# Four image layers on one core: another TensorE order in the third layer's loop, another order of mixing, convolution and loads in the last stage

## The chip, the cores and the metric

The kernel runs on one core of one Trainium2 chip. The metric is the time of one execution in microseconds (us); the median of three executions of the kernel before is 4027.63 us (4027.61 to 4030.76). The rows below come from one profiled execution. PE is the TensorE matmul, DVE VectorE, ACT ScalarE, POOL GpSimd, SP the engine that issues nearly all DMAs.

## The reference, cut to what matters

Four residual layers over x of 8 images x 32 channels x 128 x 128, float32. The change touches the third and the fourth.

```python
x = x + _L0_conv_ref(_gn(x), ...)
x = x + _L1_conv_ref(_gn(x), ...)
x = x + _L2_conv_ref(_gn(x), ...)   # layer 3 here: attention
x = x + _L3_conv_ref(_gn(x), ...)   # layer 4 here: global * local

# _L2: channel mean, a 5x5 difference of Gaussians, a 3x3 Sobel pair, then
#   return x * (1.0 + ALPHA * sigmoid(mag * gate_w[0] + gate_b[0]))
# _L3:
c_ft = jnp.fft.rfft2(c)
top = jnp.einsum('bixy,ioxy->boxy', c_ft[:, :, :m, :m], w1)
bot = jnp.einsum('bixy,ioxy->boxy', c_ft[:, :, -m:, :m], w2)
...
g = jnp.fft.irfft2(out_ft, s=(h, w))
l = y + conv_b          # y: a 3x3 convolution with wrapped borders
return g * l
```

## The kernel before

All five engines run one program each and wait on semaphores that count up. The order of the work on an engine is the order in which its program is written; no scheduler moves anything.

The first 3140 us (layers 1 and 2) are not touched, but for two semaphores that are merged. Then come the **tails**, a loop over t from -2 to 8 on PE and ACT (`for t in range(-2, B + 1)`), with its counterparts on DVE (over i), POOL and SP. An iteration handles three images at once: the attention of image t+1, the norm and forward DFT of image t, and the last layer's 3x3 convolution of image t-1. Its steps, for one image:

- POOL `tail_sum` (L1172) adds layer 2's result; DVE `group_stats` (L1196) takes the statistics; `group_means` (L551) and `group_vars` (L558) are PE products that sum them, between them DVE `group_deviations`; ACT `group_root` (L902) and DVE `group_scale` finish a norm, and ACT `normalise` (L908) writes the normed image into `xn3`. gn2 is the norm ahead of the attention, gn3 the one ahead of the last layer.
- PE `gray_sum` (L788) sums the channels, ACT copies the sum (L1064), PE `blur` (L749), ACT copies it (L1069), PE `sobel` (L755, L757), ACT squares and takes the root (L1078), and later the tanh (L1086); DVE `attend` (L1486, L1489) applies the attention and takes gn3's statistics.
- PE `dft_rows` (L766) and `dft_columns` (L778) transform the image; ACT `dft_out` (L1038) and `spectrum` (L1045) copy the results.
- DVE `bands` (L1512 to L1514) transposes the normed image into one of the two buffers `cpad`; POOL adds the border rows (L1185, L1186, `halo_ready`); PE `conv3` (L568) convolves it in two halves of 9 taps; a half takes all four PSUM banks 0 to 3, so ACT `conv3_out` (L1052) has to evacuate one half before the next starts. SP `bands_out` (L488) stores the result to `l3_dram`; the attended image is stored to `x3_dram` (L495).

conv3 is cut into parts of taps (`TAP_PARTS`) that are laid between the four quarters of gray_sum and of dft_rows.

Behind the loop comes the **last stage**. PE mixes the spectra of all images with the weights `wm` (L846), into banks 0 to 3, after the last convolution. ACT copies the result to `ys` (L1099), SP stores it to `spec_dram` in 32 DMAs (L522) and loads it back in another layout (L525). Then for each image ACT copies its slice (L1105), PE does the inverse DFT in two steps (L859, ACT L1110, L870), DVE multiplies with the convolution's result in `le` and adds the attended image in `xe` (L1551, L1553), and SP stores `xe` as output (L540). `xe` and `le` have two buffers each, and SP's loop takes the images in pairs: loads of both (L535, L311), then the two stores.

## Time and profile before

| | |
|---|---|
| profiled execution, its own time | 4031.34 us |
| its span | 4029.5 us |
| median of three executions | 4027.63 us |
| mean granted TensorE clock | 0.909 |
| busy: PE, DVE, POOL, ACT | 3360.5, 2853.2, 2344.2, 1851.4 us |
| DMA queue of kind instruction | 287 packets, 4.70 MB |
| layers 1 and 2 | until about 3140 us |
| tails and last convolution | 3140 to 3712 us |
| mixing of the spectra | 3712 to 3772 us |
| spectrum stored and loaded, inverse DFT, output | 3772 to 4029.5 us |

A line of the timeline reads: start, length in us, engine, line of the program, operation, out<-in, shapes, number of instructions, and in brackets the idle time of the engine ahead of it with what ended it. "issue" there means that the engine waited for nothing that the profile shows. The profile counts a float32 matmul twice. Granted clock 1.00 is 2.4 GHz, 0.50 is 1.2 GHz.

### The profile page before, as it was taken

What the parts mean: (1) busy time and instruction counts of PE and PEld (TensorE: products, weight loads), DVE (VectorE), ACT (ScalarE), POOL (GpSimd) and SP (SyncE); (2) the same over time, 40 slices, a digit from 0 to 9 for tenths busy, and PEclk for the clock granted to TensorE, in tenths of its full rate; (3) what the DMA queues carried; (4) which work ended last, traced back from release to release, by engine and by line L of the source; (5) the groups of instructions that cost most, each with busy time, mean ns of one, the idle gap of its engine ahead of it and who ended that gap; (6) DMA issues with size and microseconds to landing.
All of it is one profiled execution on the core that took longest, in us unless ns stands there. A gap on an engine that the chain in (4) does not pass through costs nothing.

```text
span 4029.5 us, 90064 instructions
## 1 busy us (share of the span) xinstructions
PE 3360.5 (83%) x32900; PEld 1182.2 (29%) x32900; DVE 2853.2 (71%) x3513; ACT 1851.4 (46%) x2702; POOL 2344.2 (58%) x1131
## 2 busy tenths in 40 slices
PE   5669999569999999999999999999999568776444
PEld 2334444212212222222222222222222345454433
DVE  3652554379989989899899999899999654542034
ACT  0115556445555545555455555555555455552010
POOL 0000000069999999999999999999999432301000
PEclk9889999779999999999999999999999778787555
DMA  7574898666656666666656666666666544415487
GB/s 161 126 157 97 168 184 171 154 143 153 143 137 155 150 143 144 147 148 152 144 138 155 151 144 148 139 157 149 149 148 159 135 126 117 137 54 117 104 213 205
DMA packets 495588, 586.47 MB, mean 146 GB/s; under 512 B 72354, under 2 KB 335138, under 8 KB 489819
## 3 DMA queue, kind: packets, MB, share of 16 engines
q1 hardware_dynamic: 484596, 563.66, 61.0%
q10 hardware_dynamic: 10560, 16.93, 1.7%
q8 instruction: 287, 4.70, 0.5%
q14 instruction: 145, 1.19, 0.1%
HBM read 409.91 MB, written 184.54 MB: 148 GB/s over the span
## 4 chain that ended last, share of the span: by engine, by line
POOL 30%; PE 29%; issue 27%; DMA 4%; DVE 4%; ACT 3%; SPq 2%; ACTq 0%; POOLq 0%; DVEq 0%
POOL arena L1153 26%; PE ps L568 7%; PE ps L609 7%; PE ps L616 4%; PE ps L680 3%; DMA arena<-l_dram 2%; PE ps L766 2%; POOL arena L1141 2%; ACT arena L908 1%; PE ps L870 1%; PE ps L662 1%; PE ps L788 1%; DVE arena L1551 1%; PE ps L846 1%; DMA arena<-x_dram 1%
## 5 line engine op out<-in xcount | busy, mean ns | idle before, releaser
L1153 POOL TENSOR_TENSOR arena<-arena 128x1024 f32<-128x1024 f32 x896 | 1932.1, 2198 | 553.6 <-ACT arena L1011 553.6
L1464 DVE TENSOR_TENSOR arena<-ps,arena 128x1024 f32<-128x1024 f32 x1792 | 2107.0, 1219 | 203.9 <-PE ps L662 172.7
L680 PE MATMUL ps<-arena,w_mix 128*32 128x512 f32 x10752 | 1437.9, 607 | 79.6 <-POOL arena L1153 79.6
L1011 ACT ACTIVATE arena<-ps 128x1024 f32<-128x1024 f32 x896 | 918.8, 1025 | 1025.1 <-PE ps L672 1014.2
L662 PE MATMUL ps<-arena,sel 48*128 48x512 bf16 x3584 | 701.9, 385 | 24.3 <-issue 15.6
L662 PEld LDWEIGHTS ps<-arena,sel 48*128 48x128 bf16 x3584 | 190.1, 93 | 944.4 <-issue 936.0
L568 PE MATMUL ps<-arena,w_conv 32*32 32x512 f32 x9216 | 368.6, 674 | 74.8 <-POOL arena L1186 34.5
L672 PE MATMUL ps<-norms,opw 57*128 57x512 bf16 x1792 | 348.1, 384 | 49.1 <-ACT arena L943 17.5
L680 PEld LDWEIGHTS ps<-arena,w_mix 128*32 128x32 f32 x10752 | 214.3, 108 | 467.5 <-issue 467.5
L908 ACT ACTIVATE arena<-arena,nmr,rstd 128x128 f32<-128x128 f32 x768 | 300.5, 481 | 33.0 <-DVE arena L1514 30.4
L609 PE MATMUL ps<-arena,circ 128*128 128x512 f32 x640 | 288.0, 595 | 14.4 <-ACT arena L922 14.4
L1185 POOL COPY arena<-arena 32x130 f32<-32x130 f32 x32 | 39.1, 1221 | 373.2 <-DVE arena L1514 372.2
L568 PEld LDWEIGHTS ps<-arena,w_conv 32*32 32x32 f32 x9216 | 169.3, 109 | 216.5 <-issue 130.2
L672 PEld LDWEIGHTS ps<-norms,opw 57*128 57x128 bf16 x1792 | 101.7, 93 | 435.3 <-issue 429.9
L1551 DVE TENSOR_TENSOR arena<-arena,ps 128x512 f32<-128x512 f32 x64 | 43.7, 682 | 253.2 <-DMA arena<-l_dram 210.0
L1136 POOL TENSOR_TENSOR arena<-arena 128x1024 f32<-128x1024 f32 x62 | 133.1, 2146 | 95.9 <-ACT arena L952 95.9
L616 PE MATMUL ps<-arena,circ 128*128 128x512 f32 x384 | 176.3, 594 | 0.0
L609 PEld LDWEIGHTS ps<-arena,circ 128*128 128x128 f32 x640 | 120.3, 189 | 167.0 <-issue 167.0
L1196 DVE BATCH_NORM_STATS2 st<-arena 128x6 f32<-128x128 f32 x768 | 156.6, 279 | 7.1 <-POOL arena L1172 4.9
L870 PE MATMUL ps<-k,arena 64*128 64x128 f32 x512 | 59.9, 422 | 111.5 <-DVE arena L1551 111.5
L1129 POOL TENSOR_TENSOR col<-col,powers 128x1 f32<-128x1 f32 x8 | 4.4, 552 | 243.4 <-DVE col L1252 243.4
L1392 DVE TENSOR_TENSOR arena<-arena 128x512 f32<-128x512 f32 x64 | 44.3, 693 | 143.0 <-ACT arena L927 141.0
(151 smaller groups left out, 2223.9 us busy)
## 6 DMA issues: line engine op xcount, KB each, us to landing
arena<-pad SPq DMA_DIRECT2D x768, 260.0 KB, 7.7
split_dram<-arena SPq DMA_DIRECT2D x64, 768.0 KB, 3.6
arena<-split_dram SPq DMA_DIRECT2D x1536, 32.0 KB, 3.1
x_dram<-arena SPq DMA_DIRECT2D x16, 2048.0 KB, 7.9
l_dram<-arena SPq DMA_DIRECT2D x128, 256.0 KB, 3.9
arena<-l_dram SPq DMA_DIRECT2D x32, 1024.0 KB, 14.8
arena<-x_dram SPq DMA_DIRECT2D x16, 2048.0 KB, 14.0
pad<-arena SPq DMA_DIRECT2D x8, 2080.0 KB, 16.6
```

The source lines that it names most:

```text
L568: m = pe.matmul(ps[C * j:C * j + C, bank + g, :], weights[C * g:C * g + C, dy, dx, :], tile[C * g:C * g + C, r:r + CR, dx:dx + W], start=t ...
L609: m = pe.matmul(ps[:, n % 2, :], circ[:, d, :], yp[h % 2][:, 4 * n:4 * n + 4, 4 - d:4 - d + W], start=d == 0, stop=d == 4)
L616: m = pe.matmul(ps[:, 2 + n % 2, :], circ[:, 5 + d, :], yp[h % 2][:, 4 * n:4 * n + 4, 4 - d:4 - d + W], start=d == 0, stop=d == 2)
L662: m = pe.matmul(ps[:, 2 * (n % 2) + e, :], sel[ROWS2 * e:ROWS2 * e + SPLIT_ROWS, u % GROUP, :], split[ROWS2 * e:ROWS2 * e + SPLIT_ROWS, pa ...
L672: m = pe.matmul(ps[:, POOL_BANK + e, :], opw[ROWS2 * e:ROWS2 * e + KROWS, SPREAD[c], :], norms[ROWS2 * e:ROWS2 * e + KROWS, buf, half, :]. ...
L680: m = pe.matmul(ps[C * g:C * g + C, SUM + chunk % 2, :], w_mix[:, s, :], ring[:, (first + g // 2) % size, NPX * (g % 2):NPX * (g % 2) + NP ...
L908: m = nc.scalar.activation(tile[:, c, :], src[:, c, :], ACT.Identity, scale=rstd[:, gn.slot + n % 2, c:c + 1], bias=nmr[:, gn.slot + n % 2 ...
L1011: nc.scalar.activation(ring_p[:, slot, :], ps[:, POOL_BANK:POOL_BANK + 2, :].rearrange("p a n -> p (a n)"), ACT.Tanh).then_inc(tanh_p, 1)
L1136: nc.gpsimd.tensor_tensor(rest, tt, hml[:, 0, :], ALU.subtract).then_inc(rows_r, 1)
L1153: nc.gpsimd.tensor_tensor(slot, slot, pixels(chunk % 2, SPREAD[n // 2], n % 2), ALU.mult).then_inc(prod_p, 1)
L1196: m = nc.vector.bn_stats(st[:, c, :], tile[:, c, :])
L1464: nc.vector.tensor_tensor(slot, weights, pixels(par, ONCE[n // 2], n % 2), ALU.mult).then_inc(prod_d, 1)
```

## The change

1. In the tails' loop on PE the first half of an iteration holds conv3 of image t-2, second half (`conv3(t - 2, 1)`), where it held image t-1, first half; the second half of the iteration holds image t-1, first half. The taps are cut 3+3+3 and end ahead of the fourth quarter, where they were cut 2+2+2+3 with the last behind it.
2. `group_means` of gn3 stands ahead of blur, `group_vars` between blur and sobel; they stood behind blur and behind sobel.
3. ACT's `conv3_out` and SP's `bands_out` follow that order; SP issues `x1_in` for a later image ahead of the stores of the convolution's first half, and the weights `wm` at the start of the last iteration but one.
4. Mixing stands ahead of the two halves of image 7's convolution and writes banks 4 to 7. conv3_out of image 7 stands on ACT behind the copies of the mixed spectrum, and PE waits for it ahead of the inverse DFT.
5. The spectrum is stored by 8 DMAs. `xe` and `le` have three buffers each, at new addresses; the loads of images 0 and 1 and `x3` of image 2 are issued ahead of the spectrum's store. Behind each output store come `l3_in(b + 3)` and then `x3_in(b + 2)`.
6. SP's and DVE's last loops are unrolled. bias0_loaded and w3_loaded are merged into const_loaded and shift_loaded.

```diff
-        ys = part(37640, 2048).rearrange("p (a b m) -> p a b m", a=8, b=B)
+        ys = part(37512, 2048).rearrange("p (a b m) -> p a b m", a=8, b=B)
...
-        xe = [planes(0), planes(24704)]
-        le = [planes(4096), planes(16384)]
+        xe = [planes(0), planes(20480), planes(24576)]
+        le = [planes(4096), planes(16384), planes(32068)]
...
             for t in range(B):
+                if t == B - 1:
+                    weights_in()
                 sp.wait_ge(x3_done, 4 * (t + 1))
                 sp.dma_start(x3_dram[t], xd[t % 3]).then_inc(x3_stored[t % 3], 16)
-                if t >= 1:
-                    bands_out(t - 1, 0)
+                if t >= 2:
+                    bands_out(t - 2, 1)
...
+            for half in range(2):
+                sp.wait_ge(l3_stored[half], 64 * (B - 2))
+            sp.wait_ge(x3_stored[(B - 3) % 3], 16 * ((B - 3) // 3 + 1))
+            l3_in(0)
+            l3_in(1)
+            sp.wait_ge(gn3.out, 4 * B)
+            sp.wait_ge(x3_stored[(B - 1) % 3], 16 * ((B - 1) // 3 + 1))
+            x3_in(0)
+            sp.wait_ge(bands_ready, B)
+            sp.wait_ge(dfth_mm, 4 * B)
+            x3_in(1)
+            bands_out(B - 2, 1)
+            sp.wait_ge(conv3_mm, 2 * (B - 1))
+            x3_in(2)
...
+            for half in range(HALVES):
+                bands_out(B - 1, half)
+            for half in range(2):
+                sp.wait_ge(l3_stored[half], 64 * B)
+            l3_in(2)
+
+            for b in range(B):
+                sp.wait_ge(out_done, START + 8 * (b + 1))
+                sp.dma_start(image(out, b), xe[b % 3]).then_inc(out_stored[b % 3], 16)
+                if b + 3 < B:
+                    l3_in(b + 3)
+                if 1 <= b and b + 2 < B:
+                    sp.wait_ge(out_stored[(b - 1) % 3], START + 16 * ((b - 1) // 3 + 1))
+                    x3_in(b + 2)
...
-            TAP_PARTS = ((0, 1), (2, 3), (4, 5), (6, 7, 8))
+            TAP_PARTS = ((0, 1, 2), (3, 4, 5), (6, 7, 8))
             for t in range(-2, B + 1):
                 for n in range(4):
                     if 0 <= t + 1 < B:
                         gray_sum(t + 1, n)
-                    if t >= 1:
-                        conv3(t - 1, 0, TAP_PARTS[n])
...
+                    if t >= 2 and n < 3:
+                        conv3(t - 2, 1, TAP_PARTS[n])
...
                 for n in range(4):
-                    if t >= 1:
-                        conv3(t - 1, 1, TAP_PARTS[n])
+                    if 1 <= t < B and n < 3:
+                        conv3(t - 1, 0, TAP_PARTS[n])
...
             pe.wait_ge(dftw_copy, 3 * B)
+            mix_spectrum()
+            for half in range(HALVES):
+                conv3(B - 1, half, range(TAPS))
             pe.wait_ge(conv3_evac, 2 * B)
...
+            for half in range(HALVES):
+                conv3_out(B - 1, half)
             act.wait_ge(spec_loaded, 16)
```

PE's program in iteration t = 6, from the gray sums (L788 before, L811 in the changed kernel; the order counts a float32 matmul once), before:

```order
1699 L788 MATMUL ps<-arena,ident 128x128 x8
1700 L568 MATMUL ps<-arena,w_conv 32x512 x32
1701 L788 MATMUL ps<-arena,ident 128x128 x8
1702 L568 MATMUL ps<-arena,w_conv 32x512 x32
1703 L788 MATMUL ps<-arena,ident 128x128 x8
1704 L568 MATMUL ps<-arena,w_conv 32x512 x32
1705 L788 MATMUL ps<-arena,ident 128x128 x8
1706 L568 MATMUL ps<-arena,w_conv 32x512 x48
1707 L749 MATMUL ps<-gray,k 128x128 x5
1708 L551 MATMUL ps<-st,k 128x32 x2
1709 L755 MATMUL ps<-dog,k 128x128 x2
```

and after:

```order
1683 L811 MATMUL ps<-arena,ident 128x128 x8
1684 L591 MATMUL ps<-arena,w_conv 32x512 x48
1685 L811 MATMUL ps<-arena,ident 128x128 x8
1686 L591 MATMUL ps<-arena,w_conv 32x512 x48
1687 L811 MATMUL ps<-arena,ident 128x128 x8
1688 L591 MATMUL ps<-arena,w_conv 32x512 x48
1689 L811 MATMUL ps<-arena,ident 128x128 x8
1690 L574 MATMUL ps<-st,k 128x32 x2
1691 L772 MATMUL ps<-gray,k 128x128 x5
1692 L581 MATMUL ps<-dev,k 128x32 x2
1693 L778 MATMUL ps<-dog,k 128x128 x2
```

The convolution (L568, now L591) ends ahead of the last gray sum, and gn3's mean (L551, now L574) stands ahead of blur (L749, now L772).

PE's program from the columns of image 7's DFT (L778 before) to the last loop, before:

```order
1732 L778 MATMUL ps<-k,arena 32x32 x64
1733 L568 MATMUL ps<-arena,w_conv 32x512 x288
1734 L846 MATMUL ps<-cs,arena 32x16 x1024
1735 L850 UNCONDITIONAL_BRANCH
1736 L850 ISA
```

and after:

```order
1711 L801 MATMUL ps<-k,arena 32x32 x64
1712 L591 MATMUL ps<-arena,w_conv 32x512 x144
1713 L867 MATMUL ps<-cs,arena 32x16 x1024
1714 L591 MATMUL ps<-arena,w_conv 32x512 x288
1715 L878 UNCONDITIONAL_BRANCH
```

One half of a convolution (image 6's second) now stands ahead of mixing (L846, now L867), and the two of image 7 behind it.

SP's issues from the last store of `x3_dram`, before:

```order
595 L495 DMA x_dram<-arena 128x4096
596 L488 DMA l_dram<-arena 128x1x512 x8
597 L513 DMA arena<-in_w1r 32x32x64 x4
598 L513 DMA arena<-in_w1i 32x32x64 x4
599 L513 DMA arena<-in_w2r 32x32x64 x4
600 L513 DMA arena<-in_w2i 32x32x64 x4
601 L488 DMA l_dram<-arena 128x1x512 x8
602 L522 DMA spec_dram<-arena 32x256 x32
603 L525 DMA arena<-spec_dram 32x8192
604 L531 UNCONDITIONAL_BRANCH
```

and after:

```order
598 L513 DMA x_dram<-arena 128x4096
599 L488 DMA l_dram<-arena 128x1x512 x8
600 L311 DMA arena<-l_dram 64x32x128 x4
601 L504 DMA arena<-x_dram 128x4096 x2
602 L488 DMA l_dram<-arena 128x1x512 x4
603 L504 DMA arena<-x_dram 128x4096
604 L545 DMA spec_dram<-arena 32x4x256 x8
605 L548 DMA arena<-spec_dram 32x8192
606 L488 DMA l_dram<-arena 128x1x512 x8
607 L311 DMA arena<-l_dram 64x32x128 x2
608 L557 DMA out<-arena 128x32x128
```

The weights stand ahead of this piece now; five image loads stand ahead of the spectrum's store, and image 7's bands and `l3` of image 2 behind the spectrum's load.

## Rows read from the trace of the kernel before

**Rows 1.** Timeline, PE, iteration t = 3 (start, us, what; idle before in brackets)

```profile
3383.30 3.56 PE L568 MATMUL ps<-arena,w_conv 32*32 32x512 f32 x64 [2.84 <-POOL arena L1186]
...
3395.31 2.05 PE L788 MATMUL ps<-arena,ident 128*128 128x128 f32 x16
...
3409.59 3.24 PE L766 MATMUL ps<-k,arena 128*128 128x64 f32 x16 [2.50 <-ACT arena L908]
3412.76 4.08 PE L568 MATMUL ps<-arena,w_conv 32*32 32x512 f32 x64
...
3423.39 3.40 PE L568 MATMUL ps<-arena,w_conv 32*32 32x512 f32 x96
...
3428.56 0.58 PE L558 MATMUL ps<-dev,k 128*128 128x32 f32 x4
```

**Rows 2.** Timeline, ACT, the same iteration

```profile
3400.73 2.12 ACT L1052 ACTIVATE arena<-ps,bias 128x1024 f32<-128x1024 f32 x2 [3.07 <-PE ps L568]
...
3425.49 1.28 ACT L902 ACT_TABLE_LOAD   x1
3429.41 0.23 ACT L902 ACTIVATE root<-sd 128x32 f32<-128x32 f32 x1 [2.64 <-DVE sd L1216]
```

**Rows 3.** Timeline, DVE, where iterations t = 3 and 4 begin

```profile
3365.25 8.02 DVE L1512 STREAM_TRANSPOSE arena<-arena 128x4096 f32<-128x4096 f32 x1
...
3430.17 8.03 DVE L1512 STREAM_TRANSPOSE arena<-arena 128x4096 f32<-128x4096 f32 x1
```

**Rows 4.** Timeline, all engines, iteration t = 1: gn3's statistics and its normalise

```profile
3252.90 6.27 DVE L1196 BATCH_NORM_STATS2 st<-arena 128x6 f32<-128x128 f32 x32
...
3276.46 2.02 ACT L908 ACTIVATE arena<-arena,nmr,rstd 128x128 f32<-128x128 f32 x5
```

**Rows 5.** Timeline, all engines, from image 7's statistics to mixing

```profile
3637.31 6.33 DVE L1196 BATCH_NORM_STATS2 st<-arena 128x6 f32<-128x128 f32 x32
...
3656.65 6.26 ACT L908 ACTIVATE arena<-arena,nmr,rstd 128x128 f32<-128x128 f32 x16 [0.65 <-DVE nmr L1223]
...
3678.98 2.12 PE L778 MATMUL ps<-k,arena 128*32 128x32 f32 x128 [0.68 <-ACT arena L1038]
...
3698.25 10.86 PE L568 MATMUL ps<-arena,w_conv 32*32 32x512 f32 x288 [2.21 <-ACT arena L1052]
...
3712.24 1.96 PE L846 MATMUL ps<-cs,arena 32*32 32x16 f32 x122 [3.13 <-DMA arena<-in_w2i]
```

**Rows 6.** Timeline, PE: two bursts of layer 1's convolution, two of mixing

```profile
203.90 4.43 PE L568 MATMUL ps<-arena,w_conv 32*32 32x512 f32 x127 [1.45 <-issue]
212.54 4.47 PE L568 MATMUL ps<-arena,w_conv 32*32 32x512 f32 x66 [4.21 <-issue]
...
3721.28 2.06 PE L846 MATMUL ps<-cs,arena 32*32 32x16 f32 x128 [2.51 <-issue]
...
3751.24 2.06 PE L846 MATMUL ps<-cs,arena 32*32 32x16 f32 x128 [1.69 <-issue]
```

**Rows 7.** Timeline, all engines, from the spectrum's store to image 1's first product

```profile
3773.99 14.91 SPq L522 DMA_DIRECT2D spec_dram<-arena  x32
...
3798.08 1.04 ACT L1105 COPY arena<-arena 32x1024 f32 x1 [24.11 <-DMA arena<-spec_dram]
...
3806.34 4.41 PE L870 MATMUL ps<-k,arena 64*128 64x128 f32 x32
...
3815.06 0.69 DVE L1551 TENSOR_TENSOR arena<-arena,ps 128x512 f32<-128x512 f32 x1 [134.21 <-DMA arena<-l_dram]
...
3832.01 0.69 DVE L1551 TENSOR_TENSOR arena<-arena,ps 128x512 f32<-128x512 f32 x1 [3.16 <-PE ps L870]
```

**Rows 8.** Last stage: image 2's first product; a stretch (last: clock, DMA share, GB/s); landing

```profile
3871.11 0.69 DVE L1551 TENSOR_TENSOR arena<-arena,ps 128x512 f32<-128x512 f32 x1 [25.27 <-DMA arena<-l_dram]
...
3904.60:3943.00 38.40, 11.46 (x156) 10.43 (x158) 10.18 (x16) 1.22 (x3) 0.00 (x0) 0.50 1.08 272
...
out<-arena SPq DMA_DIRECT2D x5, 2048.0 KB, 8.7
```

More of the change, by code:

```diff
@@ L289, in four_layers @@
         wm_loaded, spec_mm, spec_copy, spec_stored, spec_loaded = (once(n) for n in ("wm_loaded", "spec_mm", "spec_copy", "spec_stored", "spec_loaded"))
-        xe_loaded, le_loaded, out_stored = two("xe_loaded", sem), two("le_loaded", sem), two("out_stored", sem)
+        xe_loaded, le_loaded, out_stored = ([sem(f"{n}{i}") for i in range(3)] for n in ("xe_loaded", "le_loaded", "out_stored"))
         slice_done, idfth_mm, idfth_copy, idftw_mm, out_mul, out_done = (sem(n) for n in (
@@ L520, in _ @@
                 for q in range(4):
-                    for xx in range(4):
-                        sp.dma_start(spec_dram[MODES * t + 4 * q + xx],
-                                     ys[C * q:C * q + C, 4 * t + xx, :, :].rearrange("p b m -> p (b m)")).then_inc(spec_stored, 16)
-            sp.wait_ge(spec_stored, 16 * KX)
+                    first = MODES * t + 4 * q
+                    sp.dma_start(spec_dram[first:first + 4].rearrange("x o m -> o x m"),
+                                 ys[C * q:C * q + C, 4 * t:4 * t + 4, :, :].rearrange("p x b m -> p x (b m)")).then_inc(spec_stored, 16)
@@ L541, in _ @@
-            for par in range(2):
-                sp.wait_ge(out_stored[par], START + 16 * B // 2)
+            for half in range(HALVES):
[11 more added lines that the diff above has]
+                    x3_in(b + 2)
@@ L544, in _ @@
+            for b in range(B - 3, B):
+                sp.wait_ge(out_stored[b % 3], START + 16 * (b // 3 + 1))
         @block.tensor
@@ L570, in conv @@
                 return m
[L572 removed]
+            pe.wait_ge(const_loaded, 32)
             pe.wait_ge(init_done, 1)
@@ L817, in _ @@
                 if 0 <= t + 1 < B:
-                    sobel(t + 1)
+                    blur(t + 1)
                 if 0 <= t < B:
                     group_vars(gn3, t)
+                if 0 <= t + 1 < B:
+                    sobel(t + 1)
                 for n in range(4):
-                    if t >= 1:
-                        conv3(t - 1, 1, TAP_PARTS[n])
+                    if 1 <= t < B and n < 3:
+                        conv3(t - 1, 0, TAP_PARTS[n])
                     if 0 <= t < B:
@@ L1064, in _ @@
                     nc.scalar.copy(gray[:, 2:W + 2], ps[:, 5, 0:W]).then_inc(gray_done, 1)
-                if t >= 1:
-                    conv3_out(t - 1, 0)
+                if t >= 2:
+                    conv3_out(t - 2, 1)
                 if 0 <= t + 1 < B:
@@ L1090, in _ @@
                     dft_out(t, 3)
-                if t >= 1:
-                    conv3_out(t - 1, 1)
+                if 1 <= t < B:
+                    conv3_out(t - 1, 0)
                 if 0 <= t < B:
```

111 lines of the change are left out of this document (49 added, 62 removed).

## The prediction

> **What bounds the kernel now.** I read the page's busy shares by slice first: the first 3140 us are two layers whose code stays as it is, so only the last 890 us can move. There I read the chain of waits and then each engine's timeline.
>
> In the tails the iterations repeat every 64.92 us, counted between two starts of DVE's transposes in bands [rows 3]. No engine is full. PE starts cold, waits 2.84 us for image t-1's border rows from POOL [rows 1], and ends its first half with a part of the convolution behind the last gray sum. ACT evacuates that convolution (2.12 us) ahead of its copies for blur and sobel [rows 2], and the norm of the attended image, gn3, waits behind all this. So the loop is one ring: bands, gray sums with convolution, evacuation, sobel, gn3, DFT rows with convolution, gn2, bands.
>
> Between tails and output lies one serial string: two halves of image 7's convolution, mixing, the spectrum through DRAM, slices. PE mixes for 59.4 us, from 3712.24 [rows 5] to 2.3 us ahead of the spectrum's store at 3773.99 [rows 7] (ACT's copies). That is no arithmetic: a burst of 128 rows takes 2.06 us, then PE stands 1.69 us at "issue" [rows 6], so one burst costs 3.75 us. The page lists a queue of kind instruction, 287 packets and 4.70 MB (in the table above), 16 KB each, and I take the gaps for waits on such a packet.
>
> In the last stage DVE waits 25 us for data once in each pair of images [rows 8], and PE and ACT wait for DVE. When data is there, an image takes 16.95 us [rows 7].
>
> **The change part by part.** Times are counted from the start of bands in an iteration.
>
> *Steady iterations, t = 2 to 6.* The last gray sum ended at 3397.36 [rows 1]; conv3_out began at 3400.73 [rows 2]. Now that sum has 96 more counted matmuls ahead of it (3.40 us warm [rows 1]), less the 2.84 us for border rows that are long there, so it ends 0.56 us later, and I take 0.4, since PE warms up sooner without that pause. But conv3_out starts 0.35 us behind it and no more 3.37 us: net 2.6 us earlier, and so are sobel and gn3. With the mean and variance ahead of sobel, the root no longer waits for them: 0.2 us. Together 2.8 us. The second half has the first DFT quarter where it was against normalise (3409.59), then 192 counted matmuls of convolution and not 224 up to gn2's variance. But they sit differently: 32 more ahead of the third quarter's end in each of two parts (1.1 us each: at 1.2 GHz 64 take 4.08 us, later 96 take 3.40 [rows 1]), and none behind it. Before, the variance (3428.56 [rows 1]) released the root at 3429.41 [rows 2]; now ACT does, which loads two tables behind the third quarter and is ready at 3426.77 [rows 2], 17.2 us after the first quarter's start. 17.2 + 2.2 = 19.4 us against 19.8 before: 0.4 us more. An iteration gains some 3.2 us, five 16.0 us. Bounds: 0, if another wait takes over; 6.3, if PE, which now rests 1.6 us and not 2.50 ahead of the first quarter [rows 1], keeps 2.4 GHz there (quarter 2.0 us and not 3.24, 96 matmuls 3.4 and not 5.2).
>
> *Iteration 1* has no convolution in its first half any more. gn3's statistics end at 3259.17 and normalise starts at 3276.46, 17.3 us later [rows 4]. What remains of that is mean, blur, two ACT copies, sobel and root, 5.7 us worked out from the same instructions elsewhere in the trace. Gain 11.6, with the second half's share 12.0 us.
>
> *Iteration 7* convolves in its first half what is long there, while DVE still takes statistics. Statistics end at 3643.64, normalise starts at 3656.65, 13.0 us later [rows 5]; mean, deviations, variance, table and root need 5.9: gain 7.1. Its second half loses 32 counted matmuls: 1.1. Together 8.2 us.
>
> *Mixing starts earlier.* Between the end of the DFT's columns (3681.10) and mixing's start lie 31.1 us of border rows and two halves of convolution [rows 5]. One half of 10.86 us remains: 20.3 us. The weights are issued some 9 us into iteration 7 and lie there by 40 us; mixing begins at about 63, so they hide (before, mixing waited 3.13 us for the last of them [rows 5]).
>
> Mixing so begins 12.0 + 16.0 + 8.2 + 20.3 = **56.5 us** earlier.
>
> *Mixing under load.* New beside it: five image loads of 2.1 MB and a store of 1 MB, 11.5 MB, at 272 GB/s [rows 8] 42 us, of which about 36 fall into mixing. Its instructions come by the same DMA engines. In layer 1, where the DMAs were nearly full, two bursts of 128 lie 8.64 us apart [rows 6]; under the last weights and stores a burst of mixing lay 2.06 + 2.51 = 4.57 us behind the one before [rows 6]. In 36 us, bursts of 4.57 us lose 36 x (1 - 3.75/4.57) = 6 us, bursts of 8.64 lose 20. I take 12, nearer the middle, since the image loads are as dense as layer 1's: **-12 us**.
>
> The Trainium skill (Runtime: NRT & Kernel Launch, Instruction fetch mechanics) says that crossing a 16 KiB block is mostly hidden. The trace does not agree for these short matmuls, 1.69 us stand open at each; by the rule the term would be 0 and the time 12 us less.
>
> *From the spectrum's store on.* Let R be that store's start, 3773.99 before; the kernel ended at R + 255.5. Now PE convolves image 7 from R - 2.3: 12.1 us (10.86 and 1.3 for a cold start, 64 in 3.56 against 96 in 3.40 [rows 1]), evacuation 2.2, 10.9, evacuation 2.2: R + 25.1. The spectrum is back sooner: eight issues, 0.47 to 0.8 us each (14.91/32 [rows 7]; the stores of a quarter MB cost the latter), and not 14.91 us. So the convolution decides. Before, the slice was copied at R + 24.1 and the first product was possible 12.7 us later, at 3810.75 [rows 7]; it waited for `le` until R + 41.1. Now it is due at R + 25.1 + 12.7 = R + 37.8, images 0 and 1 loaded. An image done 13.8 us later (16.95 less the 3.16 for PE [rows 7]): image 0 at R + 51.6, 1 at 68.6, 2 at 85.6.
>
> From then on DMA decides. One store and four loads, 10.5 MB, took 38.4 us at 272 GB/s, DMA share 1.08 [rows 8], so an image's 6.3 MB cost 23.1 us, above 16.95. The batch behind image b is its store, l3 of b+3, x3 of b+2; the first has no x3. It starts at 51.6 and takes 15.4. Then four of 23: 68.6 to 91.6, 114.6, 137.6, 160.6, and one without l3 to 176. x3 of image 3 is there at 91.6, x3 of 6 at 160.6, image 6 done at 160.6 + 1.5 + 13.8 = 176, image 7 at 193, its store landed (8.7 [rows 8]) at **R + 202**. Gain 255.5 - 202 = **53.5 us**. Bounds: 181 were DMA free (17 us an image), 230 did an image cost the 29 us that it takes now.
>
> *Hidden.* Three x3 stores and bands that move in SP's queue have 15 us and more of slack: POOL reads its loads 18 us into an iteration. Merged semaphores wait for transfers that are long done. Unrolled loops need a few instruction packets on DVE and SP, 0 to 5 us, inside the range.
>
> **The sum**: 56.5 - 12 + 53.5 = 98.0 us. The profiled execution took 4031.34 us (span 4029.5), 3.7 above the median. Against the median: 4027.6 - 98.0 = 3929.6, I say 3930.
>
> **The rivals.**
>
> *The last stage stays at its pace.* Loads and stores now alternate image by image, and SP waits for a store ahead of x3. If an image then costs 29 us, the output ends at R + 230, the time is 3958. For it: x3(b+2), which is needed next, queues behind l3(b+3), which is not. Against: DMA never runs dry, since a batch is issued 7 us and more ahead of the end of the one before.
>
> *Mixing starves.* 20 us and a few for the half of convolution beside the loads: 3940 to 3950. For it: an x3 row of 16 KB is one piece. The Trainium skill (DMA: Bandwidth & Descriptors, Queues, rings and completion order) has each DMA engine take turns between queues a packet at a time, so an instruction packet waits for a whole one of the loads; layer 1's 8.64 us would agree. Against: the stores and weights beside mixing cost only 0.82 us a burst [rows 6].
>
> *The tails keep 64.9 us*, since a chain that I took for slack (ACT's copies, DVE's second statistics) is next: no 16.0, 3946.
>
> *PE stays at 2.4 GHz in the second half*: 15 us more gain, 3915.
>
> *Slower than before*: five batches would have to cost 100 us more than I count, 43 us an image, that is 6.3 MB at 146 GB/s. It would need stores and loads of neighbouring images to hinder each other that much; the stretch of [rows 8] holds a store and loads at 272. Above 4028 only if it falls under that 146.
>
> *The change does not do what it says*: the program order shows it in place, so this has no chance of its own.
>
> **How the numbers follow.** The forecast, 3930 with 12 us to both sides, 0.50; last stage at its pace 0.14; mixing starves 0.14; faster clock 0.12; tails unchanged 0.07; slower 0.03. The range 3902 to 3960 takes in all but the slow case and combinations of two. Some 0.2% (8 us) is what a measurement of this kernel tells from no change; all cases but one lie far below: faster 0.96, same 0.01, slower 0.03.
>
> **What would show it.** Tails: starts of bands 61.7 us apart; no wait for POOL at the first convolution. Normalise of gn3 6 us behind its statistics in iterations 1 and 7. Mixing: total 71 us and not 59.4, its gaps longer while x3 loads run. First product 38 us behind the spectrum's store, with no wait for `le`. From image 3 on, first products 23 us apart, DMA share near 1. The prediction is wrong where images come every 17 or 29 us, or mixing takes over 85.

## The result, and the profile after

The changed kernel takes 3923.6 us (median of 4 runs, 3922.26 to 3929.7) against 4027.93 us before, measured again beside it: a ratio of 0.9742, 95% interval 0.9726 to 0.9759. The forecast was 3930, with 3902 to 3960 as range. The profiled execution took 3922.26 us with a span of 3920.1, 109.4 less than the span before.

The page of the changed kernel, in parts: busy times, the slices of PE's clock and of the DMAs, the instruction queue.

```profile
PE 3338.9 (85%) x32900; PEld 1184.0 (30%) x32900; DVE 2855.7 (73%) x3513; ACT 1849.5 (47%) x2702; POOL 2341.5 (60%) x1131
...
PEclk9899999879999999999999999999999967888665
DMA  6574898566656656666666666666666664535589
...
q8 instruction: 287, 4.70, 0.5%
```

The matmuls (32900), the instruction packets (287) and the bytes are what they were. PE is busy 3338.9 us and not 3360.5, which is 21.6 of the 109.4 us; the rest are waits that went. The last two of the 40 slices move 191 and 251 GB/s, where 213 and 205 stood before.

Timeline of PE in iteration 3, which answers to [rows 1] (start, us, what, idle before and its releaser):

```profile
3356.82 3.57 PE L811 MATMUL ps<-arena,ident 128*128 128x128 f32 x15 [9.19 <-ACT arena L936]
...
3360.53 4.41 PE L591 MATMUL ps<-arena,w_conv 32*32 32x512 f32 x96
...
3381.40 3.41 PE L591 MATMUL ps<-arena,w_conv 32*32 32x512 f32 x96
3386.36 2.00 PE L789 MATMUL ps<-k,arena 128*128 128x64 f32 x16 [1.56 <-ACT arena L936]
3388.29 3.41 PE L591 MATMUL ps<-arena,w_conv 32*32 32x512 f32 x96
```

In the tails no matmul waits for POOL any more. The pause ahead of the first DFT quarter is 1.56 us and not 2.50; that quarter takes 2.00 us and not 3.24, and 96 matmuls behind it 3.41 us, where 64 took 4.08. The granted clock (third number from the end of a line below) of the convolution behind the quarter says the same, in the kernel before, in the changed one, and in iteration 4 of the changed one:

```profile
3412.80:3416.80 4.00, 4.00 (x66) 1.01 (x65) 0.00 (x0) 3.67 (x9) 0.00 (x0) 0.50 1.21 202
...
3388.36:3391.70 3.34, 3.34 (x98) 1.40 (x97) 0.71 (x4) 3.34 (x9) 0.00 (x0) 1.00 1.19 206
...
3448.00:3453.00 5.00, 5.00 (x98) 1.90 (x97) 0.78 (x5) 4.65 (x12) 0.00 (x0) 0.66 1.21 197
```

So behind the first quarter PE keeps 2.4 GHz in iteration 3, where it had fallen to 1.2 GHz before. It does not in every iteration: in the last line the 96 matmuls take 5.01 us at a mean of 0.66, though the pause ahead of the quarter was 1.55 us there too. The transposes in bands, which answer to [rows 3], where iterations 2, 3 and 4 begin:

```profile
3345.37 8.04 DVE L1542 STREAM_TRANSPOSE arena<-arena 128x4096 f32<-128x4096 f32 x1
3406.43 8.03 DVE L1542 STREAM_TRANSPOSE arena<-arena 128x4096 f32<-128x4096 f32 x1
3466.01 8.02 DVE L1542 STREAM_TRANSPOSE arena<-arena 128x4096 f32<-128x4096 f32 x1
```

Iterations 2 to 6 take 58.0, 61.1, 59.6, 57.5 and 55.9 us, where 65.0, 64.9, 64.9, 64.9 and 60.3 stood. The spread is new. In iteration 3 PE stops for 2 us within the third part of the convolution:

```profile
3397.84 2.17 PE L591 MATMUL ps<-arena,w_conv 32*32 32x512 f32 x43 [2.04 <-issue]
```

Every profile that has both the new order of the convolution and its cut into 3+3+3 has such a stop in iteration 3, of 0.45 to 2.67 us, and nearly all have one in iteration 4. What causes it was not tried.

Mixing in PE's timeline (five of the first bursts, and one later), for [rows 6], and the issues of the spectrum's store and load in SP's queue:

```profile
3648.28 2.05 PE L867 MATMUL ps<-cs,arena 32*32 32x16 f32 x128 [6.36 <-issue]
3657.78 2.05 PE L867 MATMUL ps<-cs,arena 32*32 32x16 f32 x128 [7.45 <-issue]
3663.99 2.05 PE L867 MATMUL ps<-cs,arena 32*32 32x16 f32 x128 [4.16 <-issue]
3669.93 2.06 PE L867 MATMUL ps<-cs,arena 32*32 32x16 f32 x128 [3.89 <-issue]
3676.14 2.05 PE L867 MATMUL ps<-cs,arena 32*32 32x16 f32 x128 [4.16 <-issue]
...
3690.85 2.05 PE L867 MATMUL ps<-cs,arena 32*32 32x16 f32 x128 [1.70 <-issue]
```

```profile
3719.86 4.75 SPq L545 DMA_DIRECT2D spec_dram<-arena  x8
3726.41 0.32 SPq L548 DMA_DIRECT2D arena<-spec_dram  x1
```

Stretches (us, busy time and count of PE, PEld, DVE, ACT, POOL; clock, DMA share, GB/s):

```profile
3640.00:3680.00 40.00, 12.29 (x743) 11.36 (x728) 0.00 (x0) 2.12 (x2) 0.00 (x0) 0.58 0.98 270
3680.00:3720.00 40.00, 23.88 (x1379) 21.46 (x1395) 0.00 (x0) 2.31 (x8) 0.00 (x0) 0.50 0.02 5
...
3745.00:3770.00 25.00, 19.64 (x297) 18.32 (x301) 10.49 (x16) 4.40 (x8) 0.00 (x0) 0.57 0.71 127
...
3820.00:3840.00 20.00, 11.40 (x192) 10.53 (x192) 8.44 (x14) 3.07 (x5) 0.00 (x0) 0.59 1.16 274
```

While loads fill the DMAs (share 0.98), PE stands 4 to 7.5 us between bursts of 128; in the second half of mixing the DMAs are idle (0.02) and the gaps are what they were. First products of images 0, 1, 2, 3 and 4 on DVE, for [rows 7, 8]:

```profile
3756.02 0.69 DVE L1580 TENSOR_TENSOR arena<-arena,ps 128x512 f32<-128x512 f32 x1 [124.07 <-PE ps L898]
...
3775.36 0.69 DVE L1580 TENSOR_TENSOR arena<-arena,ps 128x512 f32<-128x512 f32 x1 [5.41 <-PE ps L898]
...
3794.71 0.69 DVE L1580 TENSOR_TENSOR arena<-arena,ps 128x512 f32<-128x512 f32 x1 [5.40 <-PE ps L898]
...
3815.58 0.69 DVE L1580 TENSOR_TENSOR arena<-arena,ps 128x512 f32<-128x512 f32 x1 [6.93 <-DMA arena<-x_dram]
...
3837.68 0.69 DVE L1580 TENSOR_TENSOR arena<-arena,ps 128x512 f32<-128x512 f32 x1 [8.34 <-DMA arena<-x_dram]
```

The last two of the stretches lie in the last stage; from 3820 to 3840 the DMAs are full (share 1.16). The wait of 25 us in each pair of images is gone; 7 to 8 us in each of images 3 to 6 remain, for x3.

### The profile page after: what moved, and what is told of

Same layout as the page of the kernel before. It is cut to its first block, busy times and chain, and to the rows that moved or that the text cites. A ratio compares the mean times of both kernels' runs of the same rounds, so it can differ in the third digit from the quotient of the medians.

```text
span 3920.1 us, 89862 instructions
## 1 busy us (share of the span) xinstructions
PE 3338.9 (85%) x32900; PEld 1184.0 (30%) x32900; DVE 2855.7 (73%) x3513; ACT 1849.5 (47%) x2702; POOL 2341.5 (60%) x1131
## 4 chain that ended last, share of the span: by engine, by line
PE 30%; POOL 29%; issue 28%; DVE 5%; ACT 4%; DMA 2%; SPq 1%; ACTq 0%; POOLq 0%; DVEq 0%
POOL arena L1183 27%; PE ps L591 8%; PE ps L632 7%; PE ps L639 4%; PE ps L703 3%; POOL arena L1171 2%; ACT arena L936 2%; PE ps L789 1%; PE ps L811 1%; DVE arena L1542 1%; PE ps L685 1%; PE ps L898 1%; PE ps L867 1%; DMA arena<-x_dram 1%; DMA w_conv<-in_conv_w 1%
## 5 line engine op out<-in xcount | busy, mean ns | idle before, releaser
L591 PE MATMUL ps<-arena,w_conv 32*32 32x512 f32 x9216 | 354.0, 650 | 42.6 <-issue 34.3
L591 PEld LDWEIGHTS ps<-arena,w_conv 32*32 32x32 f32 x9216 | 179.1, 107 | 178.8 <-issue 125.5
L811 PE MATMUL ps<-arena,ident 128*128 128x128 f32 x512 | 78.8, 319 | 70.0 <-ACT arena L936 69.9
```

The costliest lines, as they stand in the source:

```text
L591: m = pe.matmul(ps[C * j:C * j + C, bank + g, :], weights[C * g:C * g + C, dy, dx, :], tile[C * g:C * g + C, r:r + CR, dx:dx + W], start=t ...
```

## The experiments

Each kernel's one profile was cut at the same marks: T, the first transposes in bands, bands(0), where iteration 1 begins; bands(1) and bands(6), where iterations 2 and 7 begin; the first matmul of mixing; R, the first store of the spectrum; the end. All in us, worked out as differences of such rows; the median is of all runs of the kernel:

| kernel | T | iteration 1 | iterations 2 to 6, mean | bands(6) to mixing | mixing to R | R to end | T to end | median |
|---|---|---|---|---|---|---|---|---|
| before | 3235.2 | 65.1 | 64.0 | 92.0 | 61.8 | 255.5 | 794.3 | 4027.9 |
| changed | 3233.9 | 53.5 | 58.4 | 60.5 | 79.9 | 200.2 | 686.2 | 3923.6 |
| changed_again | 3245.2 | 53.5 | 59.3 | 60.2 | 77.5 | 197.0 | 684.3 | 3928.6 |
| tails_only | 3240.7 | 53.1 | 58.2 | 90.7 | 62.2 | 256.8 | 753.9 | 3993.4 |
| last_only | 3232.8 | 65.2 | 64.0 | 61.7 | 76.9 | 201.9 | 725.8 | 3960.2 |
| norm_order_undone | 3230.8 | 51.0 | 58.9 | 60.4 | 81.0 | 200.0 | 686.8 | 3920.6 |
| four_parts | 3234.2 | 55.4 | 60.5 | 60.5 | 78.5 | 201.1 | 698.0 | 3941.7 |
| before_filler | 3240.7 | 63.7 | 62.9 | 87.5 | 61.1 | 255.8 | 782.3 | 4021.4 |
| quiet_mixing | 3236.2 | 53.2 | 58.3 | 59.6 | 60.5 | 216.9 | 681.4 | 3922.8 |
| l_in_mixing | 3244.6 | 53.5 | 58.8 | 60.5 | 70.4 | 196.5 | 674.6 | 3918.8 |
| x_in_mixing | 3240.3 | 53.2 | 58.9 | 59.6 | 67.1 | 203.9 | 678.4 | 3921.1 |
| three_in_mixing | 3241.9 | 53.5 | 58.6 | 60.3 | 76.7 | 197.5 | 680.7 | 3918.8 |
| two_buffers | 3232.4 | 53.5 | 58.5 | 60.4 | 76.4 | 203.1 | 685.7 | 3925.1 |
| combined | 3236.8 | 51.5 | 59.2 | 60.9 | 70.9 | 194.0 | 673.1 | 3909.7 |

T varies by 14 us between profiles, though ahead of it only the order of a few instructions differs. So differences of a few us are read from T on, and a median alone tells little below 10 us.

**The changed kernel again.** The kernel unchanged, beside the last three.

> The changed kernel itself, measured again beside the next three: 3920 to 3925. Its profile gives the distance from the first transposes in bands to the end once more; 686 us as in the first profile, if the spread between runs of some us comes from the two layers ahead of that point.

3928.61 us (3922.47 to 3935.03, 5 runs), above what was expected; T to end 684.3, 1.9 less than in the first profile, while T itself came 11.3 us later. The difference between the two profiles does come from ahead of T. Its parts are not that steady: iteration 3 took 65.3 us here and 61.1 there (a stop of 2.67 us, and PE at half rate behind it), while mixing was 2.4 and R to end 3.2 us shorter. So the mean iteration is good to some 1 us, mixing and R to end to some 3.

**The tails alone.** In short:

```
+            for half in range(HALVES):
+                conv3(B - 1, half, range(TAPS))
             pe.wait_ge(wm_loaded, 16 * 16)
             pe.wait_ge(dftw_copy, 3 * B)
+            pe.wait_ge(conv3_evac, 2 * B)
             mix_spectrum()
-            for half in range(HALVES):
-                conv3(B - 1, half, range(TAPS))
-            pe.wait_ge(conv3_evac, 2 * B)
```

and the buffers, loads and output loop of the kernel before.

> The changed PE, ACT and SP order of the tails alone; image 7's convolution ahead of mixing, two buffers and the output loop as in the kernel before. In the changed kernel's profile the DFT's columns of image 7 end 51.3 us earlier than before, and here three halves of convolution follow (6's second, 7's two, some 35 us with their evacuations) instead of two and the wait for border rows (31.1 us). So mixing starts some 47 us earlier, takes 59.4 us, and all behind it is as before: 3980. Rival: part of the 51.3 us comes from the last stage's edits, such as the transfers that no more stand in SP's queue; then this gains less, 3990 or more.

3993.39 us (ratio 0.9914, 0.9896 to 0.9932): 13 us above the expected, and where the rival had it. T was 5.5 us later than before; from T on it gains 40.4. Iterations 1 to 6 gain as in the changed kernel (12.0 and 29.0), but from bands(6) to mixing only 1.3 us are left, where I had expected 6: the third half of convolution and its waits take more than I gave them. The DFT's columns end 50.4 us behind bands(6), as in the changed kernel (50.3; before 60.8), so the rival's reason does not hold; from there to mixing it is 40.4 us, where I had counted 35 and the kernel before has 31.1.

**The last stage alone.**

```
-            TAP_PARTS = ((0, 1, 2), (3, 4, 5), (6, 7, 8))
+            TAP_PARTS = ((0, 1), (2, 3), (4, 5), (6, 7, 8))
...
-                    if t >= 2 and n < 3:
-                        conv3(t - 2, 1, TAP_PARTS[n])
+                    if 1 <= t < B:
+                        conv3(t - 1, 0, TAP_PARTS[n])
```

with the rest of the tails' order as before (the second half of convolution, the norm, ACT's and SP's order).

> The order of the tails as in the kernel before, the last stage changed: mixing directly behind the DFT's columns, both halves of image 7's convolution behind it, three buffers loaded during it. 31 us less ahead of mixing, 18 more in it (77.6 us for 59.4, as the changed kernel's profile shows), 55 less from the spectrum's store on: 4028 - 68 = 3960. The two parts then sum to 116 us where both together gave 104, since the wait for image 7's border rows (7 us) and evacuations are hidden by either. Rival: the gains of the last stage hang on the tails' order (border rows late, mixing starved more): 3975 or more.

3960.18 us (ratio 0.9825, 0.9802 to 0.9848), as expected; 68.5 us from T on. With the tails' 40.4 that makes 108.9, and both together gave 108.1 and 110.0. The parts simply add; the overlap of 12 us that I expected does not exist.

**The norm's order undone.**

```
+                if 0 <= t + 1 < B:
+                    blur(t + 1)
                 if 0 <= t < B:
                     after(pe, dftw_copy, 3 * t)
                     group_means(gn3, t)
                 if 0 <= t + 1 < B:
-                    blur(t + 1)
+                    sobel(t + 1)
                 if 0 <= t < B:
                     group_vars(gn3, t)
-                if 0 <= t + 1 < B:
-                    sobel(t + 1)
```

> The changed kernel with gn3's means behind the blur and its variance behind sobel again; the convolution's halves stay where the change has them. Theory: the pause of PE ahead of the first DFT quarter grows from 1.56 us to about 2.5 us, the granted clock falls again, the quarter takes 3.2 us and not 2.0, the 96 matmuls behind it 5.2 and not 3.4: 3.3 us in each of six iterations, 3943. Rival: the clock is kept by what PE does ahead (96 instead of 64 matmuls, no wait for border rows), and the order of the norm is worth 0.2 us each: 3925.

3920.64 us (ratio 0.9738, 0.9716 to 0.9760), T to end 686.8: no difference. The theory behind 3943 falls, and the trace says why; PE in iteration 3:

```profile
3375.94 3.40 PE L591 MATMUL ps<-arena,w_conv 32*32 32x512 f32 x96
3380.79 2.00 PE L789 MATMUL ps<-k,arena 128*128 128x64 f32 x16 [1.45 <-ACT arena L936]
```

The pause is 1.45 us with the old order and 1.56 with the new: 96 matmuls (3.40 us) stand ahead of the quarter where 64 (2.35 us) stood. What shortened the pause is the new cut of the convolution, not the order of the norm. In iteration 1 the new order even loses 2.4 us (53.5 against 51.0).

**Four parts.** The next run changes only that cut.

```
-                    if 1 <= t < B and n < 3:
-                        conv3(t - 1, 0, TAP_PARTS[n])
+                    if 1 <= t < B:
+                        conv3(t - 1, 0, ((0, 1), (2, 3), (4, 5), (6, 7, 8))[n])
```

> The changed kernel, with the convolution half beside the DFT in four parts (64, 64, 64, 96 matmuls) as before the change instead of three of 96; the other half keeps its three. Theory: PE's pause ahead of the first DFT quarter sets the clock. 64 instead of 96 matmuls there make it 2.5 us and not 1.56, the granted clock falls, the quarter takes 3.2 us and not 2.0 and the part behind it runs at half speed: 3 us an iteration, 3940. Rival: the clock is kept by what comes earlier (no wait for border rows, 96 matmuls in the first half): the pause is 2.5 us, the quarter 2.0 us all the same, and the time 3925.

```profile
3386.73 2.35 PE L591 MATMUL ps<-arena,w_conv 32*32 32x512 f32 x64
3391.68 3.67 PE L789 MATMUL ps<-k,arena 128*128 128x64 f32 x16 [2.60 <-ACT arena L936]
3395.28 3.71 PE L591 MATMUL ps<-arena,w_conv 32*32 32x512 f32 x64
```

3941.69 us (ratio 0.9794, 0.9767 to 0.9820), 12 to 14 us more from T on. In all five steady iterations the pause is 2.60 or 2.61 us and the quarter takes 3.67 or 3.68; in the changed kernel the pause is 1.55 or 1.56 and the quarter 2.00, though what PE does in the first half is the same in both. An iteration costs 1.2 to 2.1 us more on the mean, less than the 3 expected. It is not less everywhere: iterations 2 and 5 take 61.3 and 61.4 us, 3.3 to 4.3 more than in the two profiles of the changed kernel. But iterations 3 and 4 are hardly longer, since the changed kernel loses time there by its stops at "issue" and four_parts has none, and iteration 6 costs 1 us more.

**More work in the kernel before.**

```
+                if 1 <= t < B - 1:
+                    for _ in range(16):
+                        pe.matmul(ps[:, 6, 0:W], sobm[:, 0, :], dog[:, 0:W], start=True, stop=True)
```

> The kernel before, with 16 matmuls of 128 columns added behind gn3's variance in iterations 1 to 6; they write a PSUM bank that the first DFT quarter overwrites, so this is added work alone. Theory: the pause ahead of that quarter shrinks from 2.5 to about 1.5 us, PE keeps 2.4 GHz, the quarter takes 2.0 us and not 3.2, the part behind it half the time: 2 to 3 us an iteration less by more work, 4012 to 4016. Rival: the clock falls for what came earlier (the wait for border rows), and nothing changes: 4028.

```profile
3408.52 3.82 PE L823 MATMUL ps<-dog,k 128*128 128x128 f32 x32
3412.27 2.35 PE L568 MATMUL ps<-arena,w_conv 32*32 32x512 f32 x64
3414.55 2.00 PE L766 MATMUL ps<-k,arena 128*128 128x64 f32 x16
3416.47 2.35 PE L568 MATMUL ps<-arena,w_conv 32*32 32x512 f32 x64
```

4021.43 us (ratio 0.9986, 0.9974 to 0.9998), and 12.0 less from T on. The theory had 4012 to 4016, the rival 4028. The added matmuls count double, as 32, and take 3.82 us, so they fill the whole pause of 2.5 us and 1.3 us more; the quarter takes 2.00 us and not 3.2, and the part behind it 2.35 and not 4.1, both at a granted clock of 1.00 (from 3414.55 to 3418.80). An iteration is 1.15 us shorter with 3.8 us more work in it, where 2 to 3 us were expected. From bands(6) to mixing it is 4.5 us shorter too, though nothing was added in iteration 7; its pause is 1.44 us and not 1.96, and its first quarter 2.00. An exact fill was not tried. The wait for border rows (2.84 us) is still in this kernel, and the clock holds all the same, so that wait was not the cause. What these runs do not tell apart is the length of the pause and the amount of work just ahead of it: each run that changed one changed the other.

**No loads in mixing.** All of l3_in(0), l3_in(1), x3_in(0) to x3_in(2) moved behind the spectrum's load:

```
             sp.dma_start(arena[0:KX, 8192:8192 + C * B * 2 * MODES], spec_dram.rearrange("x o m -> x (o m)")).then_inc(spec_loaded, 16)
+            for half in range(2):
+                sp.wait_ge(l3_stored[half], 64 * (B - 1))
+            l3_in(0)
+            x3_in(0)
+            l3_in(1)
+            x3_in(1)
+            x3_in(2)
```

> The changed kernel, but the loads of images 0 and 1 and of x3 of image 2 are issued behind the spectrum's load and not during mixing. Theory: mixing's 18 extra us are instruction packets that wait behind the loads' packets. Then mixing takes 59 to 62 us, the spectrum's store comes some 17 us earlier; the 42 us of loads then run from 9 us behind that store to 51 us behind it, ahead of the first image's end, so only the convolution of image 7 pays some us for its own instructions: 3911. Rival 1: mixing is slow for another reason (what precedes it, the weights, the stores of bands): 3925 to 3940. Rival 2: the last stage is bound by bytes, so what mixing gives the stage takes back: 3922.

```profile
3646.53 2.05 PE L867 MATMUL ps<-cs,arena 32*32 32x16 f32 x128 [1.70 <-issue]
...
3810.77 0.69 DVE L1580 TENSOR_TENSOR arena<-arena,ps 128x512 f32<-128x512 f32 x1 [18.32 <-DMA arena<-x_dram]
```

3922.82 us (ratio 0.9742, 0.9724 to 0.9760). Mixing falls from 79.9 to 60.5 us: its extra time was the loads, shown. But from R on it takes 216.9 us, 16.7 more: image 3 waits 18.3 us for its x3, whose load stands behind those of convolved images 3 and 4. The second rival came true; of the 17 to 19 us saved in mixing only 3 to 5 stay from T on.

**Two loads of either kind in mixing.** In l_in_mixing only l3_in(0) and l3_in(1) stay there, in x_in_mixing only x3_in(0) and x3_in(1).

> The changed kernel, with only the convolved images 0 and 1 (4.2 MB) loaded during mixing and the x3 of images 0 to 2 issued behind the spectrum's load. Theory: 42 us of loads cost mixing 19.4 us (77.2 against 57.8 with none), so 15.5 us of loads cost some 7; and the last stage is bound by bytes (with all loads behind the spectrum it took 217 us from the spectrum's store on), of which this moves 15.5 us into mixing, whose second half leaves the DMAs idle. So mixing 65 us, end at the store's start + 201, 3909. Rival: the last stage gives back whatever mixing gains, here too: 3921. Rival on packets: the 512-byte rows of these loads disturb the instructions more, mixing 70 us or more.

> The same with the x3 of images 0 and 1 (4.2 MB, packets of 16 KB) loaded during mixing and the convolved images behind the spectrum's load. Theory that only the time of the loads counts: as with the convolved images, mixing 65 us and 3909. Theory that an instruction packet waits for whole packets of the loads: the large packets cost more, mixing 68 to 72 us and 3913 to 3917, and the run beside it less.

3918.76 us (ratio 0.9732, 0.9703 to 0.9761) and 3921.09 us (the same ratio and interval). From T on 674.6 and 678.4, 10 to 12 and 6 to 8 less than the changed kernel. Two DMA views of 10 us of mixing, 3655 to 3665 in l_in_mixing (GB/s by slice, packets) and 3650 to 3660 in x_in_mixing (packets):

```profile
GB/s 188 178 172 166 176 178 186 205 236 152 156 145 145 145 215 276 299 299 281 223 201 203 199 199 195 193 201 195 186 193 186 190 211 217 248 279 285 277 264 215
DMA packets 4081, 2.09 MB, mean 209 GB/s; under 512 B 32, under 2 KB 4080, under 8 KB 4080
```

```profile
DMA packets 744, 3.44 MB, mean 344 GB/s; under 512 B 94, under 2 KB 94, under 8 KB 597
```

The convolved image travels in packets of some 512 bytes at some 200 GB/s. In the second view 147 packets are over 8 KB, the rows of x3, among smaller ones of the stores, at 344 GB/s. Mixing's gaps reach 5.81 us under the former and 4.44 under the latter, and it takes 9.9 and 6.6 us more than with none: the large packets are not the worse ones. The changed kernel has both: gaps of 6.4 and 7.5 us while the DMAs move some 200 GB/s (the convolved images), then 3.9 to 4.2 us at 400 GB/s and more (x3). The Trainium skill (DMA: Bandwidth & Descriptors, Queues, rings and completion order) has each DMA engine take turns between queues a packet at a time, where a packet is a bundle of several descriptors. So it need not be what the profile counts as a packet, and the price that I feared, by the size of a row, the trace does not bear out. What fits all the runs is how long the DMAs are full within mixing: some 20 us for 9.9 us of loss in l_in_mixing, 11 us for 6.6 in x_in_mixing (part of its loads ran ahead of mixing), 35 us for 17 to 19 in the two profiles of the changed kernel, about half a microsecond lost for each.

**Three loads in mixing.** x3_in(0) joins the two of l_in_mixing.

> The changed kernel with three loads during mixing (convolved images 0 and 1, x3 of image 0), x3 of 1 and 2 behind the spectrum's load. No load in mixing gave 681.4 us from the first transposes to the end, two 674.6, all five 686.2. Each load costs mixing 3.9 us and spares the bytes-bound stage 7.7 us, as long as the DMAs are busy behind the spectrum. Theory: with three they still are, 671 us, time 3909. Rival: from the third on the spared bytes leave the DMAs idle until the first image is stored: 677 to 679, time 3915.

3918.81 us (ratio 0.9738, 0.9720 to 0.9756), T to end 680.7: the rival, and a little worse. Mixing pays 6.3 us for this third load, and R to end is 1 us longer: it spares nothing. The cost is not 3.9 us a load: none 60.5 us, two 67 to 70, three 76.7, four (two_buffers) 76.4, five 77.5 to 79.9.

**Two buffers.**

```
-                if b + 3 < B:
-                    l3_in(b + 3)
-                if 1 <= b and b + 2 < B:
-                    sp.wait_ge(out_stored[(b - 1) % 3], START + 16 * ((b - 1) // 3 + 1))
-                    x3_in(b + 2)
+                if b + 2 < B:
+                    l3_in(b + 2)
+                    sp.wait_ge(out_stored[b % 2], START + 16 * (b // 2 + 1))
+                    x3_in(b + 2)
```

> The changed kernel with two buffers instead of three for x3 and the convolved image, still image by image (store b, convolved image b+2, and x3 of b+2 once the store has landed); images 0 and 1 are loaded in mixing. Theory: what ended the stall of 25 us a pair is the order image by image and not the third buffer; DMA stays the bound with some 21 us an image, and only the 15 us of loads that no longer run ahead of the first product come on top, less 4 us in mixing: 3934. Rival: without the third buffer a load waits for a store and the next product for the load, 29 us an image: 3965 and more.

```profile
3832.42 0.69 DVE L1577 TENSOR_TENSOR arena<-arena,ps 128x512 f32<-128x512 f32 x1 [7.28 <-DMA arena<-x_dram]
...
3853.28 0.69 DVE L1577 TENSOR_TENSOR arena<-arena,ps 128x512 f32<-128x512 f32 x1 [6.93 <-DMA arena<-x_dram]
```

3925.07 us (ratio 0.9757, 0.9741 to 0.9774), T to end 685.7. Images come every 20.9 us; with three buffers it was 21.3. The third buffer is worth nothing that these runs can tell; what ended the stall of 25 us is that stores and loads go image by image and no more by pairs. My 3934 was too high: R to end is only 3 to 6 us longer where I had counted 15. The loads of image 2, now behind the store of image 0, still come in time for it, and then image 7 waits for its data as well (6.89 us).

**Combined.** The loads of l_in_mixing, blur ahead of the norm's means for t below 2, and:

```
-                if b + 3 < B:
-                    l3_in(b + 3)
                 if 1 <= b and b + 2 < B:
                     sp.wait_ge(out_stored[(b - 1) % 3], START + 16 * ((b - 1) // 3 + 1))
                     x3_in(b + 2)
+                if b + 3 < B:
+                    l3_in(b + 3)
```

> The changed kernel with three edits: only the convolved images 0 and 1 are loaded during mixing; in the last stage x3 of image b+2 is loaded ahead of the convolved image b+3; gn3's means stand behind the blur in the first iterations (t below 2) and ahead of it from t = 2 on. Theory: the first is worth 11.6 us (from the profiles, counted from the first transposes in bands), the third 2.4 us in iteration 1, as the run with the norm's order undone showed, the second nothing to 2 us, since bytes bound the stage and their number stays. From the first transposes to the end 671 us instead of 686, the time 3909. Rival: x3 first shortens DVE's waits of 7 to 8 us an image, and the stage with them: 3895 to 3903.

```profile
3803.51 0.69 DVE L1584 TENSOR_TENSOR arena<-arena,ps 128x512 f32<-128x512 f32 x1 [3.26 <-PE ps L902]
...
3820.95 0.69 DVE L1584 TENSOR_TENSOR arena<-arena,ps 128x512 f32<-128x512 f32 x1 [3.65 <-DMA arena<-x_dram]
3829.17 0.69 DVE L1584 TENSOR_TENSOR arena<-arena,ps 128x512 f32<-128x512 f32 x1 [2.84 <-PE ps L902]
3844.08 0.69 DVE L1584 TENSOR_TENSOR arena<-arena,ps 128x512 f32<-128x512 f32 x1 [9.52 <-DMA arena<-x_dram]
```

3909.7 us (3903.46 to 3913.47, 5 runs; ratio 0.9713, 0.9697 to 0.9728), beside 3928.61 for the changed kernel (0.9759, 0.9742 to 0.9776): the best version here. From T on it is 11 to 13 us shorter; the rest of the 19 fits T, which is 8.4 us earlier in its profile. Iteration 1 gives 2.0, mixing 7 to 9, R to end 3 to 6, where x3 first may have given 2.5 (194.0 against 196.5 in l_in_mixing, within what two profiles of one kernel differ by). Image 3 no longer waits for data, but images 5, 6 and 7 then wait 9.5, 8.4 and 6.5 us: the bytes remain, as the first theory had it.

## Why the prediction was right, point by point

The time was 6.4 us below the forecast (measured again, 1.4 below), and the mechanisms were those of the text but for PE's clock. Two terms were off, in opposite directions, by 12 and 6 us, so what looks like precision is partly luck; and 6.4 us is less than T alone varies.

- *Steady iterations*, 16.0 us: 28.0 measured (320.0 us from bands(1) to bands(6) before, 292.05 after). This step failed. The text had both ends, 0 and 6.3 us an iteration, had the pause of 1.6 us right (1.56), and then took 3.2, the value for a clock that falls. The rival "PE stays at 2.4 GHz", at 0.12, is what happened, though not without gaps: 5.6 us an iteration on the mean, 7.0 and 7.3 in iterations 2 and 5, 3.9 and 5.3 in iterations 3 and 4 with their stops. Iteration 6 was no steady one to begin with, 60.3 us and not the 64.9 that the text counted, and gained 4.5. The rival "the tails keep 64.9 us" is out. The first part of the step, convolution out of the evacuation's way and no wait for POOL, is as described, but four_parts, where PE falls to 1.2 GHz again, still gains 3.5 us an iteration on the kernel before, so the 3.2 us was a fair figure for that case.
- *With the mean and variance ahead of sobel*, 0.2 us: nothing measurable, and 2.4 us lost in iteration 1.
- *Iteration 1*, 12.0: 11.6 measured, but otherwise than said. Normalise starts 33.2 us behind bands(0) and not 41.3 [rows 4], that is 9.2 us behind the statistics, where 5.7 was worked out: 8.1 gained where 11.6 stood. The rest of the iteration gave 3.5 where 0.4 stood, its first quarter taking 2.00 us.
- *Iteration 7*, 8.2: 10.5 from bands(6) to the end of the DFT's columns (60.84 before, 50.34 after). Normalise stands 4.6 us behind the statistics, where 5.9 was counted (the first line is the last part of them):

```profile
3599.80 3.75 DVE L1226 BATCH_NORM_STATS2 st<-arena 128x6 f32<-128x128 f32 x19
...
3608.16 6.27 ACT L936 ACTIVATE arena<-arena,nmr,rstd 128x128 f32<-128x128 f32 x16 [0.65 <-DVE nmr L1253]
```

- *Mixing starts earlier*: 20.3 for the convolution ahead of it, 21.0 measured (31.1 down to 10.2). In all mixing starts 72.3 us earlier, not 56.5; 12.0 of the 15.8 between them are the steady iterations, 2.3 iteration 7, 1.2 lies ahead of T.
- *Mixing under load*, 12: 18.2 from mixing's first matmul to R (61.8 to 79.9), 15.7 in the second profile. Right mechanism (quiet_mixing takes the term to zero), inside the bounds 6 and 20, but near the upper one: the bursts under load are 5.9 to 9.5 us apart, 7.1 on the mean of 36 us, between the two figures from which the bounds came (4.57 and 8.64) and nearer the latter. The middle was taken though the only reason given, the loads' density, spoke for the upper end. The gaps were longest while the convolved images loaded, where the text had x3. That the gaps are waits for instruction packets stays a reading of the queue's 287 packets; what is shown is that the loads lengthen them. By the Trainium skill (Runtime: NRT & Kernel Launch, Instruction fetch mechanics) this term and the 1.4 to 2 us gaps would be mostly hidden; the traces do not agree: quiet_mixing, with a DMA share of 0.02 from 3650 to 3690, still shows 1.42 to 1.70 us at nearly every burst.
- *From the spectrum's store on*, 53.5: 55.3 measured, end at R + 200.2 for R + 202. The store's eight issues take 4.75 us, and the first product stands at R + 36.2, with no wait for `le`, where R + 37.8 was forecast. Behind it two sizes missed and nearly cancelled: images 0 to 2 took 19.3 us and not 16.95, and the first products of images 3 to 6 stand 20.7 to 22.1 us behind the one before and not 23.1. 6.3 MB in 21.3 us are 296 GB/s and not the 272 of [rows 8].
- *The last stage stays at its pace* and *slower than before*: neither; and two_buffers shows that the pace was set by the pairs, as the argument against that rival had it. *Mixing starves*: in part, 18 us for its 20 and more.

So the sum was 56.5 - 12 + 53.5 = 98.0, and the trace gives 72.3 - 18.2 + 55.3 = 109.4. Between the medians it is 104.3, mostly since the profiled execution of the kernel before was 3.4 us above its median and that of the changed kernel 1.3 below.

## What to carry to other kernels

Where a change cuts a pause of PE behind which its clock fell, here from 2.5 to 1.6 us, count the work behind it at both rates and give the fast one its due: a shorter wait can be worth more than its own length. Loads issued beside instruction-dense PE work are not free even if SP, DMA and PE look independent; move only as many as the later stage cannot hide, here two of five. And ask of each part of a change whether another part would do alone: three buffers and the norm's order added nothing here to what the loop's order and the convolution's cut gave.
